# The depthwise convolutions of a two-layer MetaFormer, moved from a phase of their own into the steps of the phases before and after

## What is computed

```python
# layer 0
x = x + cluster(ln_c(x))                      # clustering attention on quadrants of 64 x 64, 4 heads of 24
x = x + ffn0(ln_t(x))                         # 96 -> 384 -> 96, operands rounded to fp8 e5m2, sums to fp16
# layer 1
z = ln_c(x) * gamma + beta                    # this is x3 in the kernel
y = dw_conv(z, dw_w1, dw_b1)                  # 3 x 3, every channel by itself
y = dw_conv(y, dw_w2, dw_b2)                  # 1 x 5
y = dw_conv(y, dw_w3, dw_b3)                  # 5 x 1, this result is y3 in the kernel
x = x + conv1x1(y, pw_w) * z                  # mixes the 96 channels
x = x + ffn1(ln_t(x))
```

## Time and profile before

| | |
|---|---|
| median of 3 runs | 4172.24 us (4168.22 to 4173.44) |
| profiled execution, time | 4171.88 us |
| profiled execution, span | 4170.3 us |
| mean granted TensorE clock | 0.883 of full |
| first phase | 0 to about 2155 us |
| middle phase | 2160 to 2979 us |
| last phase | 2983 to 4170.3 us |

### The profile page before, as it was taken

The page is one execution under the profiler, slowest core; times in us unless marked ns, Lnnn a source line. Parts: engine busy times, 40 slices in busy tenths (PEclk is TensorE's granted clock), DMA queues, the critical chain, the costliest instruction groups (busy, mean ns, idle before and its releaser), DMA issues. The chain is left out here.

```text
span 4170.3 us, 80301 instructions
## 1 busy us (share of the span) xinstructions
PE 3300.1 (79%) x26660; PEld 2535.7 (61%) x26660; DVE 3017.9 (72%) x7852; ACT 2708.9 (65%) x5762; POOL 1410.4 (34%) x1892
## 2 busy tenths in 40 slices
PE   5777777777777777767769999999788888888887
PEld 5656556555565555655549999999644444444443
DVE  4888888888888888888842222222388888888887
ACT  2677777776777777767752222222188888888887
POOL 3555555555555555555310000000012211222221
PEclk8888888888888888888769999999899999999998
DMA  3133232332333323322236656666666666666662
GB/s 68 41 82 82 67 77 70 78 83 62 77 75 77 79 62 77 77 77 62 58 103 165 166 160 167 162 163 167 167 178 180 182 178 179 182 174 175 172 179 74
DMA packets 733893, 490.42 MB, mean 118 GB/s; under 512 B 420796, under 2 KB 712956, under 8 KB 721276
## 3 DMA queue, kind: packets, MB, share of 16 engines
q1 hardware_dynamic: 733564, 486.32, 44.3%
HBM read 284.42 MB, written 201.33 MB: 116 GB/s over the span
## 5 line engine op out<-in xcount | busy, mean ns | idle before, releaser
L1790 POOL TENSOR_SCALAR C_var<-C_st 128x16 f32<-128x16 f32 x64 | 13.2, 207 | 1733.2 <-DVE C_st L178 1733.2
L1331 PE MATMUL B_ps_row<-B_g,B_z 128*128 128x128 f32 x4608 | 555.9, 277 | 0.6 <-ACT B_g L1363 0.6
L1331 PEld LDWEIGHTS B_ps_row<-B_g,B_z 128*128 128x128 f32 x4608 | 532.2, 193 | 0.7 <-ACT B_g L1363 0.7
L361 ACT ACTIVATE A_h<-A_hid 128x512 f16<-128x512 f32 x768 | 426.6, 591 | 67.7 <-PE A_hid L348 64.0
L1424 DVE TENSOR_TENSOR B_mid<-B_ps_row,B_row_bias 128x512 f32<-128x512 f32 x192 | 132.7, 691 | 458.0 <-PE B_ps_row L1331 448.0
L166 POOL TENSOR_TENSOR A_rstd<-A_var,A_expo 128x16 f32<-128x16 f32 x128 | 454.2, 3548 | 23.8 <-POOL A_var L163 23.6
L178 DVE BATCH_NORM_STATS2 A_st<-A_xT 128x6 f32<-128x192 f32 x1536 | 442.9, 349 | 24.8 <-ACT A_xT L826 11.6
L1461 ACT ACTIVATE C_q<-C_xT,C_shift,C_rstd 128x96 fp8e5<-128x96 f32 x1024 | 392.0, 458 | 39.1 <-POOL C_shift L1797 38.9
L369 DVE TENSOR_SCALAR A_hq<-A_h,A_b 128x512 f16<-128x512 f16 x768 | 250.1, 363 | 198.9 <-ACT A_h L361 194.0
L307 ACT ACTIVATE C_h<-C_hid 128x1536 f16<-128x1536 f32 x256 | 370.5, 1447 | 19.1 <-PE C_hid L272 10.9
L856 ACT ACTIVATE A_xc<-A_xT,A_shift,A_rstd 128x96 f32<-128x96 f32 x1024 | 379.1, 456 | 0.0
(11 more groups left out here) (162 smaller groups left out, 7677.8 us busy)
## 6 DMA issues: line engine op xcount, KB each, us to landing
A_xq<-in_x SPq DMA_DIRECT2D x32, 1536.0 KB, 8.9
x_scratch<-A_xT SPq DMA_DIRECT2D x64, 768.0 KB, 3.2
x_scratch<-A_x3h SPq DMA_DIRECT2D x64, 768.0 KB, 5.4
B_z<-x_scratch SPq DMA_DIRECT2D x96, 512.0 KB, 5.0
y_scratch<-B_y SPq DMA_DIRECT2D x96, 512.0 KB, 3.7
C_x3q<-x_scratch SPq DMA_DIRECT2D x32, 1536.0 KB, 9.2
C_y3q<-y_scratch SPq DMA_DIRECT2D x32, 1536.0 KB, 15.6
C_xT<-x_scratch SPq DMA_DIRECT2D x64, 768.0 KB, 15.0
```

Of the source, the lines that this page charges most:

```text
L361: act.activation(self.h16[:, k % 2, j * CH:(j + 1) * CH], self.hid2[n % 2][:], ACT.Copy).then_inc(ev["h16"], 1)
L1331: m = pe.matmul(ps_row[h][:, b * P:(b + 1) * P], z[c.buf(NB)][:, h * HB + b, d:d + W], g[c.buf(2)][:, d, :], start=(d == 0), stop=(d == 2))
```

## The change

`phase_b` is gone. Its work is cut into rounds of two channels and two images. The 144 rounds of images 0 to 5 run in steps 9 to 32 of the first phase, six a step; the 48 rounds of images 6 and 7 run in the last phase, six in step -1 and two in each of units 0 to 20. The joined taps of each pair of channels are built once, in steps -4 to 7 of the first phase, four pairs a step, and kept in memory off the core (`pack_dram`); a round loads them. The taps are turned on the host, so that no engine turns them. A round has one bank for its row and its column part, one buffer for the middle and one for y3:

```diff
+PACKW = 4 * P + 1
+PAIRS = C // 2
+BUILD_FROM, BUILD_TO, BUILD_PER_STEP = -4, 8, 4
+BUILD_AT = (0, 1, 3, 4, 6, 7, 9, 10, 12, 13, 15, 16)
+CONV_FROM, CONV_PER_STEP = 9, 6
+SIX = of_step(6, lambda r: tuple(6 * (r // 2) + x for x in ((0, 1, 1, 2), (3, 4, 5, 5))[r % 2]))
+TWO = of_step(2, lambda r: tuple(8 * r + x for x in (1, 3, 5, 6)))
```

```diff
+class Conv:
...
+    def sp_load(self, sp, n):
+        u, ev = self.unit(n), self.ev
+        if begun(u - 3):
+            sp.wait_ge(ev["out"], ev.at("out", u - 3, 0))
...
+        for ch in range(2):
+            sp.dma_start(self.z(u)[:, ch, :, 1:W + 1],
+                         self.x3_dram[c0 + ch, self.images(u)].rearrange("b h w -> h b w")).then_inc(s, 16)
...
+        sp.dma_start(self.pack[u.buf(3)][:], self.pack_dram[u.n % PAIRS]).then_inc(s, 16)
+    def pe_row(self, pe, n):
+        pe.wait_ge(self.loaded[u.buf(3)], (u.round(3) + 1) * 4 * 16)
+        if begun(u - 1):
+            pe.wait_ge(ev["out"], ev.at("out", u - 1, 0))
+        for ch in range(2):
+            for b in range(2):
+                o = (2 * ch + b) * P
+                for d in range(3):
+                    m = pe.matmul(self.bank[:, o:o + P], self.z(u)[:, ch, b, d:d + W],
+                                  self.pack[u.buf(3)][:, ch, d * P:(d + 1) * P], start=(d == 0), stop=(d == 2))
+    def dve_mid(self, dve, n):
+        dve.wait_ge(ev["row"], ev.at("row", u, 0))
...
+    def pe_col(self, pe, n):
+        pe.wait_ge(ev["mid"], ev.at("mid", u, 0))
+        for ch in range(2):
+            for b in range(2):
+                m = pe.matmul(self.bank[:, o:o + P], self.mid[:, ch, b, :], self.band4(u, ch), start=True, stop=True)
+    def act_out(self, act, n):
+        act.wait_ge(ev["col"], ev.at("col", u, 0))
+        if begun(u - 1):
+            act.wait_ge(self.stored, 32 * u.n)
+        for ch in range(2):
+            m = act.activation(self.y3[:, ch], self.bank[:, 2 * ch * P:2 * (ch + 1) * P].rearrange("p (b n) -> p b n", b=2)[:, :, ::-1],
+                               ACT.Identity, bias=self.pack[u.buf(3)][:, ch, 4 * P:4 * P + 1])
...
+class Bands(Conv):
...
+    def pe_joined(self, pe, m, ch):
+        pe.wait_ge(self.band_ld[c % 3], 16 * (c // 3 + 1))
+        if ch:
+            pe.wait_ge(ev["gs"], ev.at("gs", u, 0))
+        elif begun(u - 1):
+            pe.wait_ge(ev["cb"], ev.at("cb", u - 1, 0))
+        for d in range(3):
+            pe.matmul(self.bank[:, d * P:(d + 1) * P], bd[:, d, :], bd[:, 3, :], start=True, stop=True)
+        pe.matmul(self.bank[:, 3 * P:4 * P], self.ones(), bd[:, 3, :], start=True, stop=True).then_inc(ev["g"], 1)
```

The bank and the buffers for it are taken from the first phase: the front ring has three banks in place of four, `sq` two chunks in place of four, the similarities are written over `dots`, the third normalisation has four chunks in place of eight, and x3 leaves in four quarters through two buffers. SP's list is cut into slots:

```diff
-        NSQ = 4
+        NSQ = 2
-        sim = sb("A_sim", [P, NT, HM], F32)
+        sim = dots
-        xc3 = sb("A_xc3", [P, 2, NT // 2, C], F32)
-        x3h = [sb(f"A_x3h{h}", [C, QS // 2, QS], F32) for h in range(2)]
-        front = Ring(front_uses, [ctx.enter_context(nc.psum_tensor(f"A_fbank{p}", [P, 512], F32)) for p in range(4)])
+        xc3 = sb("A_xc3", [P, 4, TPC, C], F32)
+        x3h = [sb(f"A_x3h{h}", [C, QS // 4, QS], F32) for h in range(2)]
+        front = Ring(front_uses, [ctx.enter_context(nc.psum_tensor(f"A_fbank{p}", [P, 512], F32)) for p in range(3)])
...
             def body(i):
                 p, q3 = i - 1, i + 3
+                for s in range(FFN_SLOTS):
+                    if s == 0 and p.real:
+                        store_x2(p, 1)
+                        store_x3(p, 1)
+                    if s == 2 and q3.real:
...
+                    if s == 3 and (i + 4).real and i.n >= -2:
+                        load_x(i + 4)
+                    convolve(i, 2 * s)
+                    if s == 4 and i.real:
+                        store_x2(i, 0)
+                    if s in (4, 5) and p.real:
+                        store_x3(p, s - 2)
+                    if s == 8 and i.real:
+                        store_x3(i, 0)
+                    convolve(i, 2 * s + 1)
```

In the last phase the hidden layer goes through two banks of one third each, as in the first (`SplitFeedForward`), which leaves a bank for the rounds; the loads for y3 of image 6 wait for all rounds:

```diff
-class RowFeedForward(FeedForward):
+class RowFeedForward(SplitFeedForward):
...
+        self.hid2 = [ctx.enter_context(nc.psum_tensor(phase + f"hid{p}", [P, CH], F32)) for p in range(2)]
...
+                if q.n == 24:
+                    sp.wait_ge(conv.stored, 32 * PAIRS)
...
             u = Unit(0, 0, 4, NQ - 1)
-            for q in (u, u + 1):
-                load_xy(q)
-                load_t(q)
+            load_xy(u)
+            load_t(u)
+            conv.sp_load(sp, 0)
+            conv.sp_load(sp, 1)
+            load_xy(u + 1)
+            load_t(u + 1)
...
                     if i.real and s < NK:
-                        ff.pe_hidden(pe, i, s)
+                        ff.pe_hidden(pe, i, s, 0)
+                        ff.pe_hidden(pe, i, s, 1)
+                    convolve(i, 2 * s)
                     if q.real and s < NK:
                         mix(i, s)
+                    if i.real and s < NK:
+                        ff.pe_hidden(pe, i, s, 2)
```

More of the change, by code:

```diff
@@ L408, in load_ffn_weights, with of_step @@
     return out, sp_part, dve_part, cast
+PACKW = 4 * P + 1
[3 more added lines that the diff above has]
+CONV_FROM, CONV_PER_STEP = 9, 6
+EARLY, LATE = 0, 1
+def of_step(rounds, step_slots):
+    at = {}
+    for r in range(rounds):
+        for what, x in zip(("row", "mid", "col", "out"), step_slots(r)):
+            at.setdefault((what, x), []).append(r)
+    return at
+SIX = of_step(6, lambda r: tuple(6 * (r // 2) + x for x in ((0, 1, 1, 2), (3, 4, 5, 5))[r % 2]))
@@ new lines, in convolve @@
+            def convolve(i, half):
+                n = (i.n - BUILD_FROM) * BUILD_PER_STEP
+                for a in range(BUILD_PER_STEP) if i.n < BUILD_TO else ():
+                    m = n + a
+                    if half == BUILD_AT[3 * a + 1] and m + 1 < PAIRS:
+                        conv.sp_band(sp, 2 * m + 2)
+                    if half == BUILD_AT[3 * a + 2]:
+                        conv.sp_packed(sp, m)
+                        if m + 1 < PAIRS:
+                            conv.sp_band(sp, 2 * m + 3)
+                if i.n == CONV_FROM - 1 and half == 2 * NK + 1:
+                    conv_load(0)
+                    conv_load(1)
+                n = (i.n - CONV_FROM) * CONV_PER_STEP
+                for r in SIX.get(("row", half), ()) if i.n >= CONV_FROM else ():
+                    if n + r:
+                        conv.sp_store(sp, n + r - 1)
+                    conv_load(n + r + 2)
@@ L1554, in phase_c, with rounds_of @@
         HR = RB // 2
+        conv_bank = ctx.enter_context(nc.psum_tensor("C_conv_bank", [P, 512], F32))
+        conv = Conv(nc, ctx, "C_", conv_bank, PAIRS, 6, taps, pack_dram, x3_dram, y3_dram)
+        def rounds_of(i, what, half):
+            if i.n < 0:
+                return SIX.get((what, half), [])
+            return [6 + 2 * i.n + r for r in TWO.get((what, half), ()) if 6 + 2 * i.n + r < PAIRS]
         def group(plane, k):
@@ L1665, in c_turn, with convolve @@
                 m.then_inc(ev["c_full"], 1)
+            def convolve(i, half):
+                for n in rounds_of(i, "row", half):
+                    conv.pe_row(pe, n)
+                for n in rounds_of(i, "col", half):
+                    conv.pe_col(pe, n)
             def body(i):
@@ L1687, in _, with convolve @@
         def _(act):
+            def convolve(i, half):
+                for n in rounds_of(i, "out", half):
+                    conv.act_out(act, n)
             def body(i):
@@ L1851 @@
     taps[:, 4, mid - 2:mid + 3] = a["L1_conv_dw_w2"][:, 0, 0, :]
+    taps[:, 0:4] = taps[:, 0:4, ::-1].copy()
     dwb = np.stack([a["L1_conv_dw_b1"], a["L1_conv_dw_b2"], a["L1_conv_dw_b3"]], axis=1)
```

416 lines of the change are left out of this document (225 added, 191 removed).

## The result

The changed kernel takes **4524.05 us** (median of 4 runs, 4521.45 to 4536.78) against 4172.84 us (4 runs, 4168.22 to 4173.44): a ratio of 1.085, 95% interval 1.0832 to 1.0869. It is 8.5% slower where I had forecast 8.4% faster; 4524 is 564 us above the upper end of my range.

The account below looks back on a forecast made before the run. No engine bound the kernel throughout: DVE was fullest in the first phase, TensorE alone the middle, three engines level in the last. Removing 823 us and adding 30+48+180+60 and 115+5+35 gave 3820 us, range 3650 to 3960.

Parts of the forecast that it names:

- up to slot 2 of step 0: Short steps -4 to -1, joining taps: chains of 22 to 30 us partly lengthen steps of 20 to 47; +30.
- steps 0 to 7: First phase, four pairs of taps built a step: PE, VectorE and bank costs of 6 us a step; +48.
- from slot 2 of step 8 to that of 28: First phase, six rounds a step: +9 a step, to 74 us (ends 67 and 81); twenty steps, +180.
- from there to the end of the phase: Steps 29 to 32: three thinning steps about 11 each, step 32 +26 for six rounds in series; +60.
- head of the last phase: Step -1 holds six rounds, its third load queued behind others, so unit 0 starts later; +35.
- units 0 to 20: Last phase, two rounds a unit: +5.5 a unit, to 41.4 us, a third lost in existing waits; +115.
- New waits cost about +1.3: First-phase steps 9 to 28: in-order queues, one round bank and three front banks add about 1.3 us a step.
- priced at nothing: SyncE's queue: six transfers a round, loads have two rounds to land; no cost, else a few us once a round.
- Cheap rounds: Rival: full clock, rows fall into PE's waits, steps 67 us, units 39; 3630 us in all; chance 0.18.
- Banks bind: Rival: one round bank and three front banks make engines step in turn, steps 82 us; 4028 us; chance 0.16.
- Slower than before: Rival: each round's 6.0 us chain stops its phase, about 4617 us; decides from 3.7 us a round; chance 0.04.
- The rule weighed: Full first-phase step: by weight-load share (59 us) the bound is DVE's 59.8, not PE; favours the cheap-rounds rival.

Follow-up runs that it names:

- x14: The x11 kernel unchanged, timed again in five rounds against the kernel before: 3973.92 us against 4173.49, ratio 0.952.
- x4: Changed kernel with ScalarE's order exchanged in slots 7 and 8, forward-turn copies ahead of the third normalisation: 4341.0 us.
- x6: x4 with first-phase row parts in the first half of a slot moved behind the third hidden matmul: 4247.5 us.
- x7: x4 with the column part of the first round of each pair moved half a slot later: 4352.1 us.
- x9: x8 with the round's output tile kept twice in the first phase too: 4012.5 us.
- x11: x9 with the three front banks used in another order (class norms' turn and copy earlier, second forward turn in slot 7): 3973.5 us.
- x12: x2 with ScalarE's exchange of x4: 3611.2 us against 3634.9.
- x5: x4 with the round's output tile kept twice in the last phase alone: 4262.1 us.
- x8: The edits of x5, x6 and x7 together: 4128.2 us, against 4181.4 for the kernel before on that chip.
- x2: Changed kernel without any round (row and column parts, copies, loads and stores left out), output not the reference's: 3634.9 us.
- x1: Kernel before with three front PSUM banks in place of four, no convolution moved: 4267.1 us against 4174.5.

## Why the prediction was wrong

The sum, term by term, in us of span against before (x14 beside it; boundaries as in the timelines, the even pace of before taken as (1954.17 - 140.40) / 28 = 64.78 and 36.0 a unit):

```
term                                   forecast   after    x14
middle phase                             -823      -823    -823
up to slot 2 of step 0                    +30      +100     +88
steps 0 to 7                              +48      +142     +99
from slot 2 of step 8 to that of 28      +180      +547    +211
from there to the end of the phase        +60      +131     +77
head of the last phase                    +35       +43     +45
units 0 to 20                            +115      +219    +100
units 21 to 31                             +5        +6      +7
sum                                      -350      +364    -197
```

**The step that failed** is "New waits cost about +1.3" in the steps of the first phase; in the units it is the queue, "priced at nothing" (below). I had named the three things (round's bank, three front banks, in-order queues) and priced them as small additions to a step whose idle time would take up the rest of the work. In these runs they decide whether idle time can be used at all. In the changed kernel six rounds bring 21.9 us of TensorE and lengthen the step by 27.7; without them the step is 67.7, so my +9 should have been 2.9 + 24.8. Edits that remove no work (x4, x6 with x7, x9, x11) bring 92.5 down to 75.2, 1.2 above my 74. So 17.3 of the 18.5 us by which a step missed were order, buffers and queue, and that is shown; how they split is not additive (x12: the exchange is worth 7 us a step with rounds and none without; x7 nothing alone, and whether x14 needs it was not run). The same edits bring the end of the phase from +131 to +77, for +60. One reading behind the 1.3 was short as well: I took L746 for all bank waits of the kernel before, 1.1 us a step, where with L649 and L737 they are 2.1. (A reading without effect: POOL is busy 37.2 us of 64.9, not 37.1.)

**What was right.** The amounts: PE 69.4 at a clock of 0.88 (forecast 69.3 at 0.82), and in x14 60.7 at 0.99 (60.8 at full clock), DVE 59.8 (59.8), ACT 50.8 (52). The clock came back as supposed, from 0.82 to 0.99 (nearly all at 2.4 GHz), but only where TensorE was fed. The unit once the output tile is kept twice: 40.8 in x5, x8, x9, x11 and x14, for 41.4. The head of the last phase, +43 for +35.

**Units.** 46.4 us for 41.4. The step of the sum that failed was "Priced at nothing; without that cover a late load adds its few us once a round". I had looked at the round's loads, which have two rounds to land. It is the stores that are late: they share one output tile and stand in SyncE's queue behind the quarter loads. x5 shows 5.7 us a unit.

**Build steps and head.** +48 and +30 became +142 and +100, and stay at +99 and +88 in x14. x2 shows that the rounds have no part in it, x4 and x12 that 5 of 18 us a step are ScalarE's order. Before slot 2 of step 0 TensorE waits 51.1 us for loads of bands, which I had called "at times". Three banks in place of four are 3.7 us of a build step in x1 (68.3 for 64.6). How the some 12 us a step that stay in x4 split over banks and the work of the build was not taken apart; that cause stays open.

**The rivals.** *Cheap rounds* is out: no version came under 75. *Banks bind* had the right mechanism and not the price: alone it is 2.6 us a step (x1), with the rounds 7 for one order of ScalarE (x4), and the ring's order gave 1.7 more (x11). The Trainium skill's rule in "Perfetto Trace Analysis", section Matmuls, that groups should rotate through banks, is borne out in direction by x1; neither it nor a row of before gave its size. *Slower than before* was given 0.04 and is the side on which the result fell. Its threshold of 3.7 us a round was passed: 4.6. Its mechanism, the whole chain of a round stopping the phase, is not what the runs show: with other orders and one more tile the same rounds cost about (3973.9 - 3611.2) / 192 = 1.9 us each (x12 has the exchange of x4, but not the ring's order of x11). My argument against it, that in the middle phase TensorE hid all hand-overs, was no evidence: there a round waited for nothing but rounds.

**The rule weighed.** By the share of weight loads TensorE would have had room for the rounds, and DVE's 59.8 been the bound. In x14 DVE fills 59.8 of 75.2 us and PE 60.7: neither is the bound. The measurement sides with neither share; what is left over both is waiting.

## What to carry to other kernels

The 19.5 us of TensorE's idle time in a step were no room for 21.2 us of work while other engines' next input stood behind that work and copies that free its banks stood behind other work: price moved work at its full length first, and at less only after naming the slot that takes it up. When the work brings its own bank, tile and stores, look at the copies that free each of them and at what stands ahead of those in ScalarE's and SyncE's order; here six such edits (x4 to x7, x9 and x11), none of which removes work, turned 8.5% slower into 4.8% faster. And the length of a wait is not its price: x1 has 9.4 us a step of bank waits and pays 2.6, x7 took 3.5 us a step off the longest wait for nothing, and x4 took 6.1 us off two others for 7.2.

## What the hardware showed that I had not expected

- In the changed kernel SyncE took 6.71 to 12.40 us to issue the two stores of 128 KB of a round when a load of 1.5 MB (19 times, median 7.79) or two of 768 KB (21 times, median 7.55) had been issued right ahead, once in each of 19 steps and in each unit with rounds; behind a store of a quarter of x3 (384 KB) it took 0.88 to 4.04, and a median of 0.87 us otherwise. The queue that the work is moved past is itself a place of waiting.
- The granted clock, a mix of its levels of 1.2 and 2.4 GHz, went with the waits: with the same instructions per step it was 0.88 at a step of 92.5 us, 0.91 at 85.4, 0.95 at 76.9 and 0.99 at 75.2, and TensorE's busy time for that work fell from 69.4 to 60.7 us. A wait removed gave back twice here, once as idle time and once in the clock; 8.7 of the 17.3 us gained in a step are busy time, and in x11 all of the gain is.
